# First rows of the relation table made in the front stage, and pair members of the table's sort copied to PSUM

## The chip, the cores and the metric

The kernel runs on one core of a Trainium2 chip. The metric is device time in microseconds (us), taken over several executions; lower is better. Five engines matter: TensorE (PE, with its weight loads PEld), VectorE (DVE), ScalarE (ACT), GpSimd (POOL) and SyncE (SP). SP and POOL issue the DMAs.

## The reference

Four residual blocks are applied in turn to node features x of 6,250 nodes by 256. The part that this change touches is the first block, a sum over 200,000 edges of relation-specific products:

```
# x: (6250, 256); src, dst, edge_type: (200000,); weight: (8, 256, 256)
x1  = layernorm(x)
hx  = einsum('ni,rio->rno', x1, weight)          # one product per node and relation
msg = hx[edge_type, src]
agg = segment_sum(msg, dst, 6250)
x   = x + agg * sqrt(0.5) + h_bias + (x1 @ loop_weight) * sqrt(0.5)
# second block: graph attention over 131,072 other edges (edge_index) picks
# 2 of 4 experts per node; it needs those edges ordered by their destination
# third block: gather and sum of a sparsified table over the same 200,000 edges
# fourth block: attention over 64 slice tokens
```

`dst` comes sorted and lies denser at low node numbers. The second block's edges come unsorted, so the kernel sorts them.

## The kernel before

The program is a chain of stages, each a block of five instruction streams, one for each engine. A stage ends with a barrier of all engines, so the last engine to finish sets its end. Within a stream the order is fixed by the code; engines meet through semaphores only. Nodes are handled in NW = 49 windows of P = 128 rows. Two stages matter here.

**front** loads x in 7 runs of 7 windows, normalises it in place in `b.x` (6 windows of each run on ACT, line 268, and one on POOL, line 253), writes the normalised rows to DRAM (`rows1`, SP line 224) and loads the three matrices of weights (lines 219 and 220). DVE meanwhile turns the lists of edges into tables: it takes the lowest and highest destination of each group (lines 301 to 331), TensorE spreads these over all partitions (lines 275 and 277), and DVE derives slots and masks from them (lines 336 to 375). When a run of rows has been written, POOL clears it in `b.x` (line 258), because `b.x` later serves as accumulator. The first DIRECT = 2 windows of run 0 are left for the next stage.

**relation_table** has three jobs that run beside each other.

- The table. For each window TensorE transposes the rows (`turn`, line 740), ACT copies them to `r_xt` (790), TensorE multiplies them by the 8 relation matrices in OUTS = 4 chunks of 128x512 (`multiply`, 747), ACT evacuates each chunk into `r_stage` (798), and SP stores the window, 1 MB, into `table1` (545). The rows come back from DRAM by `bring`, but for the first two windows, which are read from `b.x`. There are 3 PSUM banks for the products.
- Early edges. For the first edges (528 tiles of 128 edges less SKIP = 128, so 400 tiles), POOL gathers 128 rows for each tile with an indirect DMA into a ring of 8 (568). A 128x128 one-hot matrix is made by DVE for even tiles (702) and by ACT for odd ones (806, 809). TensorE multiplies the two into `r_sums` (758), and after each group of 4 tiles DVE adds the sums into `b.x` and `b.counted` (`add`, 695 and 697).
- The sort of the second block's 131,072 edges, a bitonic network over `r_keys`, two SBUF tensors of 128x1024 float32 used in turn. A stage compares the lower and the upper member of each pair. `mixed_stage` (422, 423) has four instructions of 128x256, `rising_stage` (433, 434) two of 128x512; both read both members from SBUF. There are 45 mixed and 108 rising stages. Fourteen times the keys are transposed by TensorE into the PSUM tensors `r_flipped` (`flip`, 766), and DVE brings them back (655, 676).

What sets the order: TensorE goes through the 196 chunks (49 windows by 4), and after each chunk takes about two gather tiles (`tiles_at`). DVE loops over the 400 tiles and does one step of the sort at tile `step_at(n)`, every 9/5 tiles, from tile 9 on; three steps after each request for a flip hold no work while it is made. ACT goes with the chunks: copy, evacuate, one-hot for tiles 7 ahead.

Names: `Chain` counts instructions of DVE in a semaphore, and `settled` waits for all of them. `b.written[j]` is raised when run j of the rows is in DRAM, `b.weighted` when the weights are in SBUF.

## Time and profile before

| what | value |
|---|---|
| median of 3 runs | 4322.95 us (4322.5 to 4335.69) |
| the profiled execution | 4332.92 us |
| its span, first to last instruction | 4331.0 us |
| TensorE busy over the span | 3673.5 us (85%) |
| POOL busy over the span | 2853.3 us (66%) |
| VectorE busy over the span | 2720.7 us (63%) |
| front: last clearing by POOL ends | 56.7 us after the start |
| relation_table: first product of TensorE | 59.9 us |
| next stage: first instruction of POOL | 643.5 us |

The profile page gives for each group of instructions the time busy, the mean of one, and the idle time just before them with what ended it. "DMA r_ring" as releaser means that TensorE stood until gathered rows had arrived. On POOL an indirect DMA counts as busy while the engine makes its descriptors; "issue" behind it is time in which it waited for nothing that the profile shows. Start times are from the start of the span. Neighbouring matmuls overlap in the records, so a period is best taken from start to start.

### The profile page before, as it was taken

What the parts mean: (1) busy time and instruction counts of PE and PEld (TensorE: products, weight loads), DVE (VectorE), ACT (ScalarE), POOL (GpSimd) and SP (SyncE); (2) the same over time, 40 slices, a digit from 0 to 9 for tenths busy, and PEclk for the clock granted to TensorE, in tenths of its full rate; (3) what the DMA queues carried; (4) which work ended last, traced back from release to release, by engine and by line L of the source; (5) the groups of instructions that cost most, each with busy time, mean ns of one, the idle gap of its engine ahead of it and who ended that gap; (6) DMA issues with size and microseconds to landing.
All of it is one profiled execution on the core that took longest, in us unless ns stands there. A gap on an engine that the chain in (4) does not pass through costs nothing. (4 is left out here: it accounts for less than half of the span.)

```text
span 4331.0 us, 73886 instructions
## 1 busy us (share of the span) xinstructions
PE 3673.5 (85%) x19739; PEld 2738.8 (63%) x19739; DVE 2720.7 (63%) x9585; ACT 1662.1 (38%) x3894; POOL 2853.3 (66%) x2874
## 2 busy tenths in 40 slices
PE   3999987777788878887699999978769999996988
PEld 2555554454455556646588888866358888884657
DVE  8766657666544443345555455557978888886862
ACT  3444444433233333323344444436523333333320
POOL 6877777777777777772677777742667777672230
PEclk9999997878799999965899999989879999997998
DMA  7555564333444443531433333336379999993001
GB/s 260 173 202 194 201 201 118 110 111 112 118 130 131 132 123 105 164 105 35 97 67 68 68 69 68 68 106 206 121 291 384 373 375 385 365 383 88 1 1 60
DMA packets 361677, 689.27 MB, mean 159 GB/s; under 512 B 70002, under 2 KB 188160, under 8 KB 354909
## 3 DMA queue, kind: packets, MB, share of 16 engines
q0 software_dynamic: 133184, 338.60, 26.0%
q1 hardware_dynamic: 228095, 345.94, 23.4%
q8 instruction: 179, 2.93, 0.3%
q14 instruction: 219, 1.79, 0.1%
HBM read 571.95 MB, written 112.35 MB: 158 GB/s over the span
## 5 line engine op out<-in xcount | busy, mean ns | idle before, releaser
L1102 POOL DMA_INDIRECT e_ring<-table,erow x1040 | 1007.0, 968 | 317.1 <-issue 177.5
L1553 PE MATMUL e_sums<-e_ring,e_onehot 128*128 128x257 f32 x2080 | 782.4, 480 | 290.1 <-DMA e_ring<-table,erow 252.1
L2652 POOL DMA_INDIRECT t_source<-source_rows,t_index x632 | 605.2, 958 | 207.2 <-issue 156.1
L1553 PEld LDWEIGHTS e_sums<-e_ring,e_onehot 128*128 128x128 f32 x2080 | 367.3, 219 | 527.3 <-issue 311.4
L1665 POOL DMA_INDIRECT e_ring<-table,esrc x544 | 535.6, 985 | 207.4 <-issue 134.8
L568 POOL DMA_INDIRECT r_ring<-rows,esrc x400 | 454.3, 1136 | 123.1 <-issue 85.0
L1068 ACT ACTIVATE k_sign<-ramp,low 128x128 bf16<-128x128 f32 x1024 | 361.5, 395 | 443.4 <-PE e_sums L1507 425.2
L1750 PE MATMUL e_total<-e_loads,e_times 128*128 128x256 f32 x3072 | 501.9, 299 | 17.2 <-DMA e_loads<-table 11.9
L1750 PEld LDWEIGHTS e_total<-e_loads,e_times 128*128 128x128 f32 x3072 | 408.7, 190 | 68.1 <-issue 35.6
L1648 ACT ACTIVATE e_times<-e_tally 128x320 fp32r<-128x320 f32 (+4 forms) x640 | 260.0, 427 | 483.1 <-PE e_tally L1734 479.2
L2836 PE MATMUL t_raw<-big,t_w 128*128 128x256 f32 x1600 | 374.8, 388 | 19.3 <-ACT t_hidden L2671 18.7
L1337 DVE SCALAR_TENSOR_TENSOR big<-e_sums,within,big 128x257 f32 x130 | 63.0, 485 | 494.1 <-PE e_sums L1553 492.4
L747 PE MATMUL r_product<-weights,r_xt 128*128 128x512 f32 x784 | 372.5, 598 | 0.0
L2847 PE MATMUL t_out<-t_w,t_hidden 128*128 128x256 f32 x1600 | 368.1, 383 | 0.0
L1692 DVE TENSOR_SCALAR e_place<-e_rampw,ddst 128x128 bf16<-128x128 f16 (+4 forms) x1024 | 340.1, 334 | 0.0
L2836 PEld LDWEIGHTS t_raw<-big,t_w 128*128 128x128 f32 x1600 | 299.5, 192 | 64.2 <-ACT t_hidden L2671 25.7
L1690 DVE TENSOR_SCALAR e_row<-e_rampr,dsrc 128x128 bf16<-128x128 bf16 x1024 | 270.4, 266 | 97.4 <-PE e_tally L1734 86.5
L2847 PEld LDWEIGHTS t_out<-t_w,t_hidden 128*128 128x128 f32 x1600 | 297.6, 190 | 37.3
L1411 DVE TENSOR_SCALAR e_onehot<-ramp,edst 128x128 f32<-128x128 f32 x1040 | 252.1, 299 | 17.7 <-DVE d_keys L1124 0.5
L1734 PE MATMUL e_tally<-e_place,e_row 128*128 128x128 bf16 (+4 forms) x1280 | 259.7, 300 | 0.0
L758 PE MATMUL r_sums<-r_ring,r_onehot 128*128 128x257 f32 x800 | 217.0, 387 | 33.2 <-DMA r_ring<-rows,esrc 32.0
L758 PEld LDWEIGHTS r_sums<-r_ring,r_onehot 128*128 128x128 f32 x800 | 149.7, 192 | 150.7 <-issue 119.9
(564 smaller groups left out, 6467.0 us busy)
## 6 DMA issues: line engine op xcount, KB each, us to landing
e_loads<-table SPq DMA_DIRECT2D x512, 256.0 KB
table<-r_stage SPq DMA_DIRECT2D x49, 1024.0 KB
outputs<-first_outputs SPq DMA_DIRECT2D x49, 512.0 KB, 6.5
first_outputs<-t_stage SPq DMA_DIRECT2D x96, 256.0 KB
t_near<-near_rows SPq DMA_DIRECT2D x79, 256.0 KB
e_ring<-table,erow POOLq DMA_INDIRECT x1040, 2.8
table<-n_split SPq DMA_DIRECT2D x49, 256.0 KB
t_source<-source_rows,t_index POOLq DMA_INDIRECT x632
```

The lines of the kernel that those rows point to most:

```text
L568: eng.indirect_dma_start(ring[:, t % RING, 0:D], None, m["rows1"], bass.IndirectOffsetOnAxis(ap=b.esrc[:, SKIP + t:SKIP + t + 1], axis=0)) ...
L747: mm = eng.matmul(product[n % BANKS][:, :], xt[w % 2][:, k, :], b.weights[:, k, 2 * c:2 * c + 2, :].rearrange("p r o -> p (r o)"), start=( ...
L758: eng.matmul(sums[g % 2][:, 0:ACCW], onehot[t % RING][:, :], ring[:, t % RING, :], start=(t % EGROUP == 0), stop=(t % EGROUP == EGROUP - 1 ...
L1068: eng.activation(sign[t % SIGNS][:, :], b.ramp[:, 0:P], ACT.Sign, bias=b.low[:, t:t + 1], scale=1.0).then_inc(signed, 1)
L1102: eng.indirect_dma_start(ring[:, t % RING, 0:D], None, table, bass.IndirectOffsetOnAxis(ap=b.erow[:, EARLY + t:EARLY + t + 1], axis=0)).th ...
L1553: eng.matmul(sums[g % SUMS][:, 0:ACCW], onehot[t % ONEHOTS][:, :], ring[:, t % RING, :], start=(t % GROUP == 0), stop=(t % GROUP == GROUP ...
L1665: eng.indirect_dma_start(ring[:, t % RING, :, :].rearrange("p n d -> p (n d)").bitcast(F32), None, halves, bass.IndirectOffsetOnAxis(ap=b. ...
L1692: eng.tensor_scalar(place[(2 * g + two) % MARKS][:, 0:wide(g) * P], rampw[:, 0:wide(g) * P], b.ddst[:, column(tile):column(tile) + 1], Non ...
L1750: mm = eng.matmul(part(n, q), times[g % TIMES][:, q * P:(q + 1) * P], loads[:, g % AHEAD, half, :], start=False, stop=False, skip_group_ch ...
L2652: eng.indirect_dma_start(source[s][:, q, :], None, a.source_rows, bass.IndirectOffsetOnAxis(ap=index[s][:, q:q + 1], axis=0)).then_inc(gat ...
L2836: mm = eng.matmul(raw[g][:, j % 2, :], w1[:, e, k, j * P:(j + 1) * P], b.xt[:, k, bass.ds(w * P, PAIR)], start=(k == 0), stop=(k == KH - 1))
L2847: mm = eng.matmul(out[s][:, q, :], hidden[s][:, j, q * P:(q + 1) * P], w2[:, e, j, :], start=(j == 0), stop=(j == NB - 1))
```

## The change

**In front.** The two windows that are still in `b.x` are multiplied there. TensorE transposes both windows once ACT has normalised them, ACT copies them out of PSUM into `c_xt` after the first window of run 1, and TensorE makes 8 chunks of 128x512 into 5 PSUM banks: chunk 0 ahead of the two matmuls that spread the lists, chunks 1 to 7 behind them. ACT evacuates the chunks behind its last normalisation, into `stage` buffers that both stages now share. SP loads the first three windows' rows of the next stage once run 0 has been written, waits for four evacuations, stores window 0, waits for four more and stores window 1. POOL clears all of run 0, after the transposes. Some lists of the front are worked on in place (`einside` and `inside` over `erows` and `rows`, `slot` over `etype`, five small ones inside `esrc`), with a wait for all of DVE's previous instructions where an input is overwritten.

**In relation_table.** MADE = 47 windows are left, so 188 chunks; the 400 tiles are spread over these. The first evacuations wait for front's stores. The two windows cleared by DVE (line 713) fall away.

**In the sort.** Before each of the 153 stages ACT copies the upper members of all pairs, 128x512, from `r_keys` into the PSUM tensor `r_flipped0` (`halve`), and DVE compares the lower members in SBUF with that copy. The copy waits until DVE has finished the step before; DVE waits for the copy. `halve` stands in ACT's stream AHEAD = 2 tiles ahead of the tile at which DVE does the step before, behind the evacuation and the one-hot of that chunk.

```diff
+MADE = NW - DIRECT
+HELD = 3
+OUTS = RELS * D // BANK
...
+    BANKS = 5
+    CHUNKS = OUTS * DIRECT
...
+        xt = sb("c_xt", [P, DIRECT, KH, P])
...
-        einside = sb("c_einside", [EROWS, 2, EGROUP * P])
+        einside = erows.bitcast(F32)
...
+        product = [ctx.enter_context(nc.psum_tensor(f"c_product{n}", [P, BANK], F32)) for n in range(BANKS)]
...
+            eng.wait_ge(b.written[0], 16)
+            for i in range(HELD):
+                eng.dma_start(b.xw[i][:, :], m["rows1"][(DIRECT + i) * P:(DIRECT + i + 1) * P, :]).then_inc(b.brought[i], 16)
+            for w in range(DIRECT):
+                eng.wait_ge(evacuated, OUTS * (w + 1))
+                eng.dma_start(m["table1"][w * P:(w + 1) * P, :], b.stage[w][:, :]).then_inc(b.stored[w], 16)
...
-                low = DIRECT if j == 0 else RUN * j
-                eng.memset(b.x[:, low:RUN * (j + 1), :], 0.0).then_inc(emptied, 1)
+                if j == 0:
+                    eng.wait_ge(transposed, 1)
+                eng.memset(b.x[:, RUN * j:RUN * (j + 1), :], 0.0).then_inc(emptied, 1)
...
+                if w == RUN:
+                    eng.wait_ge(transposed, 1)
+                    eng.activation(xt[:, :, :, :].rearrange("p w k n -> p (w k n)"),
+                                   turned[:, :, :, :].rearrange("p w k n -> p (w k n)"), ACT.Copy).then_inc(copied, 1)
+            for n in range(CHUNKS):
+                w, c = divmod(n, OUTS)
+                eng.wait_ge(multiplied, n + 1)
+                eng.activation(b.stage[w][:, c * BANK:(c + 1) * BANK], product[n % BANKS][:, :], ACT.Copy).then_inc(evacuated, 1)
...
+            def multiply(n):
+                w, c = divmod(n, OUTS)
+                wait_if(eng, evacuated, n - BANKS + 1)
+                for k in range(KH):
+                    mm = eng.matmul(product[n % BANKS][:, :], xt[:, w, k, :],
+                                    b.weights[:, k, 2 * c:2 * c + 2, :].rearrange("p r o -> p (r o)"),
+                                    start=(k == 0), stop=(k == KH - 1))
+                mm.then_inc(multiplied, 1)
+
             eng.wait_ge(filled, FILLED)
+            eng.wait_ge(normed[0], DIRECT)
+            for w in range(DIRECT):
+                for k in range(KH):
+                    mm = eng.transpose(turned[:, w, k, :], b.x[:, w, k * P:(k + 1) * P], b.ident[:, :])
+            mm.then_inc(transposed, 1)
+            eng.wait_ge(copied, 1)
+            eng.wait_ge(b.weighted, 16 * (KH + 1))
+            multiply(0)
             eng.wait_ge(ranged, RANGED)
             eng.matmul(eacross[:, :, :, :].rearrange("p q c r -> p (q c r)"), b.ones[0:EROWS, :],
                        elaid[:, :, :, :].rearrange("r q c e -> r (q c e)"), start=True, stop=True).then_inc(spread, 1)
             eng.matmul(across[:, :, :, :].rearrange("p q c r -> p (q c r)"), b.ones[0:GROWS, :],
                        laid[:, :, :, :].rearrange("r q c e -> r (q c e)"), start=True, stop=True).then_inc(spread, 1)
+            for n in range(1, CHUNKS):
+                multiply(n)
...
             v.did(eng.tensor_reduce(elowest[:, :], erows[:, :, :], AX_X, ALU.min))
+            v.settled()
             v.did(eng.scalar_tensor_tensor(einside[:, :, :], erows[:, :, :], float(N), erows[:, :, :], ALU.is_lt, ALU.mult))
...
+    def halved(self):
+        self.stages += 1
+        self.v.eng.wait_ge(self.copied, self.stages)
...
+def mixed_stage(eng, keys, order, half, k, j):
 
     v = order.v
     cut = lambda t: t[:, :].rearrange("p (a u b o c) -> p a u b o c", u=2, b=1 << (k - 1 - j), o=2, c=1 << j)
     source, target = cut(keys[order.at]), cut(keys[1 - order.at])
+    above = half[:, :].rearrange("p (a u b c) -> p a u b c", u=2, b=1 << (k - 1 - j), c=1 << j)
+    order.halved()
     v.settled()
     for u in range(2):
-        first, second = source[:, :, u, :, 0, :], source[:, :, u, :, 1, :]
+        first, second = source[:, :, u, :, 0, :], above[:, :, u, :, :]
         v.did(eng.tensor_tensor(target[:, :, u, :, u, :], first, second, ALU.min))
         v.did(eng.tensor_tensor(target[:, :, u, :, 1 - u, :], first, second, ALU.max))
     order.turn()
...
+def rising_stage(eng, keys, order, half, reach):
 
     v = order.v
     cut = lambda t: t[:, :].rearrange("p (a o c) -> p a o c", o=2, c=reach)
     source, target = cut(keys[order.at]), cut(keys[1 - order.at])
+    above = half[:, :].rearrange("p (a c) -> p a c", c=reach)
+    order.halved()
     v.settled()
-    v.did(eng.tensor_tensor(target[:, :, 0, :], source[:, :, 0, :], source[:, :, 1, :], ALU.min))
-    v.did(eng.tensor_tensor(target[:, :, 1, :], source[:, :, 0, :], source[:, :, 1, :], ALU.max))
+    v.did(eng.tensor_tensor(target[:, :, 0, :], source[:, :, 0, :], above, ALU.min))
+    v.did(eng.tensor_tensor(target[:, :, 1, :], source[:, :, 0, :], above, ALU.max))
     order.turn()
...
+    AHEAD = 2
+    halves_at = {}
+    for stage_of in table_stages():
+        halves_at.setdefault(max(0, step_at(stage_of[0] - 1) - AHEAD), []).append(stage_of)
+    sorted_to = {}
...
+                eng.wait_ge(transposed, w - HELD + 1)
+                eng.dma_start(xw[w % HELD][:, :], rows[DIRECT + w]).then_inc(brought[w % HELD], 16)
...
-            for w in range(DIRECT, DIRECT + HELD):
-                eng.dma_start(xw[w % HELD][:, :], rows[w]).then_inc(brought[w % HELD], 16)
             eng.dma_start(m["scr_edst"], b.edst[:, :]).then_inc(kept, 16)
-            for w in range(NW):
+            for w in range(MADE):
                 eng.wait_ge(evacuated, (w + 1) * OUTS)
-                eng.dma_start(table[w], stage[w % 2][:, :]).then_inc(stored[w % 2], 16)
-                if DIRECT + HELD <= w + HELD < NW:
+                eng.dma_start(table[DIRECT + w], stage[w % 2][:, :]).then_inc(stored[w % 2], 16)
+                if w + HELD < MADE:
...
+            half = flipped[0]
...
-            eng.wait_ge(transposed, DIRECT)
-            eng.memset(b.x[:, 0:DIRECT, :], 0.0).then_inc(zeroed, 1)
...
-                    wait_if(eng, stored[w % 2], 16 * (w // 2))
+                    eng.wait_ge(stored[w % 2], 16 * (w // 2 + 1))
...
+            def halve(step, at, reach):
+                eng.wait_ge(sorting, sorted_to[step - 1])
+                eng.activation(flipped[0][:, :].rearrange("p (a c) -> p a c", c=reach),
+                               keys[at][:, :].rearrange("p (a o c) -> p a o c", o=2, c=reach)[:, :, 1, :],
+                               ACT.Copy).then_inc(halved, 1)
...
                     for t in tiles_at(step_of(w, c), RING - 1):
                         if t % 2 == 1:
                             match(t)
+                    for t in tiles_at(step_of(w, c), 0):
+                        for stage_of in halves_at.get(t, ()):
+                            halve(*stage_of)
+            for t in range(TILES - TAIL, TILES):
+                for stage_of in halves_at.get(t, ()):
+                    halve(*stage_of)
```

TensorE from its first instruction on. Before, front holds the two matmuls that spread the lists, and relation_table opens with the transposes of the windows in `features` (that is `b.x`):

```order
L275 MATMUL c_eacross<-c_elaid,ones 128x264
L277 MATMUL c_across<-c_laid,ones 128x392
L117 UNCONDITIONAL_BRANCH
L730 UNCONDITIONAL_BRANCH
L740 MATMUL r_turned<-ident,features 128x128 x4
L747 MATMUL r_product<-weights,r_xt 128x512 x2
```

The changed kernel's TensorE from its first instruction on:

```order
L310 MATMUL c_turned<-ident,features 128x128 x4
L301 MATMUL c_product<-weights,c_xt 128x512 x2
L316 MATMUL c_eacross<-c_elaid,ones 128x264
L318 MATMUL c_across<-c_laid,ones 128x392
L301 MATMUL c_product<-weights,c_xt 128x512 x14
L120 UNCONDITIONAL_BRANCH
L820 UNCONDITIONAL_BRANCH
L826 MATMUL r_turned<-ident,rows_in 128x128 x4
L833 MATMUL r_product<-weights,r_xt 128x512 x2
```

Four transposes and one chunk now stand ahead of the matmuls that spread the lists, and seven chunks behind them.

ACT in relation_table while the sort runs. Before (evacuation, then the two instructions of a one-hot):

```order
L798 ACTIVATE r_stage<-r_product 128x512
L806 ACTIVATE r_away<-ramp,edst 128x128
L809 ACTIVATE r_onehot<-r_away,ones 128x128
L798 ACTIVATE r_stage<-r_product 128x512
L806 ACTIVATE r_away<-ramp,edst 128x128
L809 ACTIVATE r_onehot<-r_away,ones 128x128
```

The changed kernel's ACT at the same kind of place:

```order
L899 ACTIVATE r_flipped<-r_keys 128x512
L883 ACTIVATE stage<-r_product 128x512
L891 ACTIVATE r_away<-ramp,edst 128x128
L894 ACTIVATE r_onehot<-r_away,ones 128x128
L899 ACTIVATE r_flipped<-r_keys 128x512
L883 ACTIVATE stage<-r_product 128x512
```

One copy of pair members has come in behind nearly every evacuation and one-hot.

DVE between two additions of sums, early in the sort. Before:

```order
L702 TENSOR_SCALAR r_onehot<-ramp,edst 128x128
L422 TENSOR_TENSOR r_keys<-r_keys 128x128x2
L423 TENSOR_TENSOR r_keys<-r_keys 128x128x2
L422 TENSOR_TENSOR r_keys<-r_keys 128x128x2
L423 TENSOR_TENSOR r_keys<-r_keys 128x128x2
L702 TENSOR_SCALAR r_onehot<-ramp,edst 128x128
```

The changed kernel's DVE there:

```order
L794 TENSOR_SCALAR r_onehot<-ramp,edst 128x128
L475 TENSOR_TENSOR r_keys<-r_keys,r_flipped 128x128x2
L476 TENSOR_TENSOR r_keys<-r_keys,r_flipped 128x128x2
L475 TENSOR_TENSOR r_keys<-r_keys,r_flipped 128x128x2
L476 TENSOR_TENSOR r_keys<-r_keys,r_flipped 128x128x2
L794 TENSOR_SCALAR r_onehot<-ramp,edst 128x128
```

The order is the same; the second operand now comes from `r_flipped`.

## Rows read from the trace of the kernel before

**Rows 1.** The page's costliest groups: busy, mean ns, idle before and releaser.

```profile
L568 POOL DMA_INDIRECT r_ring<-rows,esrc x400 | 454.3, 1136 | 123.1 <-issue 85.0
```

**Rows 2.** Waits in 57 to 644 us: us in total, times, longest.

```profile
PE r_sums L758 <- DMA r_ring<-rows,esrc: 32.0, 32, 2.3
...
POOL r_ring L568 <- PE r_sums L758: 37.1, 120, 0.6
```

**Rows 3.** Timeline of TensorE with a flip and a turn: start, length, then the instruction.

```profile
486.56 1.04 PE L766 MATMUL r_flipped<-ident,r_keys 128*128 128x128 f32 x8
487.43 0.60 PE L758 MATMUL r_sums<-r_ring,r_onehot 128*128 128x257 f32 x2
487.86 1.88 PE L747 MATMUL r_product<-weights,r_xt 128*128 128x512 f32 x4
489.58 1.03 PE L758 MATMUL r_sums<-r_ring,r_onehot 128*128 128x257 f32 x4
490.45 0.38 PE L740 MATMUL r_turned<-ident,r_xw 128*128 128x128 f32 x2
490.67 1.88 PE L747 MATMUL r_product<-weights,r_xt 128*128 128x512 f32 x4
```

**Rows 4.** Timeline of POOL: one gather beside line 655, one beside a stage.

```profile
288.39 0.94 POOL L568 DMA_INDIRECT r_ring<-rows,esrc  x1 [0.30 <-issue]
...
294.56 2.13 POOL L568 DMA_INDIRECT r_ring<-rows,esrc  x1 [0.30 <-issue]
```

**Rows 5.** Timeline of DVE over the same time.

```profile
287.83 1.29 DVE L655 TENSOR_TENSOR r_keys<-r_flipped,r_change 128x512 f32<-128x512 f32 x2 [6.34 <-PE r_flipped L766]
...
293.34 0.48 DVE L695 SCALAR_TENSOR_TENSOR features<-r_sums,ewithin,features 128x256 f32 x1
...
294.57 0.69 DVE L433 TENSOR_TENSOR r_keys<-r_keys 128x512 f32<-128x512 f32 x1
295.18 0.69 DVE L434 TENSOR_TENSOR r_keys<-r_keys 128x512 f32<-128x512 f32 x1
```

**Rows 6.** POOL's groups by line, 611 to 643 us and 660 to 800 us.

```profile
L568 POOL DMA_INDIRECT r_ring<-rows,esrc x20 | 19.0, 950 | 6.1 <-issue 4.3 <-PE r_sums L758 1.8
...
L1102 POOL DMA_INDIRECT e_ring<-table,erow x111 | 106.7, 962 | 33.8 <-issue 18.3 <-PE e_sums L1553 15.5
```

**Rows 7.** Timeline at the start of relation_table: TensorE's products and DVE.

```profile
59.93 3.04 PE L747 MATMUL r_product<-weights,r_xt 128*128 128x512 f32 x4
...
63.30 0.69 DVE L583 TENSOR_SCALAR r_keys<-r_ends 128x1024 int32<-128x1024 int32 x1 [2.20 <-DMA r_ends<-in_gdst_cols]
...
68.41 3.62 PE L747 MATMUL r_product<-weights,r_xt 128*128 128x512 f32 x4
...
73.03 1.88 PE L747 MATMUL r_product<-weights,r_xt 128*128 128x512 f32 x4
```

**Rows 8.** Timeline at the end of relation_table.

```profile
631.72 3.49 PE L758 MATMUL r_sums<-r_ring,r_onehot 128*128 128x257 f32 x14
...
643.51 0.13 POOL L1094 MEMSET e_ring<- 128x17 f32 x1 [7.86 <-POOLq L120]
```

**Rows 9.** Timeline of front on TensorE, DVE and POOL.

```profile
40.24 1.22 PE L275 MATMUL c_eacross<-c_elaid,ones 66*128 66x264 f32 x2 [40.24 <-DVE c_elaid L331]
...
42.98 1.17 POOL L258 MEMSET features<- 128x1280 f32 x1 [1.41 <-DMA rows<-features]
...
45.38 0.29 DVE L351 CAST c_ebasis<-c_eacross 128x132 int32<-128x132 f32 x1
...
54.85 1.88 POOL L258 MEMSET features<- 128x1792 f32 x1 [0.78 <-DMA rows<-features]
```

**Rows 10.** Timeline of the next stage's sort, in which ACT already copies pair members.

```profile
711.54 0.42 DVE L1118 TENSOR_TENSOR d_keys<-d_keys,d_half 128x256 f32<-128x256 f32 x1
712.05 0.60 ACT L1019 ACTIVATE d_half<-d_keys 128x512 f32<-128x512 f32 x1 [3.16 <-DVEq L1160]
...
712.79 0.42 DVE L1117 TENSOR_TENSOR d_keys<-d_keys,d_half 128x256 f32<-128x256 f32 x1
```

More of the change, by code:

```diff
@@ L460, in table_asked, with table_stages @@
     return asked
+def table_stages():
+    stages, step, at = [], 3, 0
+    for k in range(1, LOGF):
+        for j in range(k - 1, -1, -1):
+            stages.append((step, at, 1 << j))
+            step, at = step + 1, 1 - at
+    step, at = step + 1, 1 - at
+    for j in range(LOGF - 1, -1, -1):
+        stages.append((step, at, 1 << j))
+        step, at = step + (j > 0), 1 - at
+    for k in range(LOGF + 1, LOGE + 1):
+        for reaches in ([1 << (j - LOGF) if j >= LOGF else P << (j - 7) for j in range(k - 1, 6, -1)],
+                        [1 << j for j in range(6, -1, -1)]):
+            step, at = step + 3, 1 - at
+            for reach in reaches:
+                step += 1
+                stages.append((step, at, reach))
+                at = 1 - at
+    return stages
 def relation_table(nc, b, m):
-    OUTS = RELS * D // BANK
     BANKS = 3
@@ L488, in relation_table @@
         pb = lambda name: ctx.enter_context(nc.psum_tensor(name, [P, BANK], F32))
[L489 removed]
+        xw, stage, brought, stored = b.xw, b.stage, b.brought, b.stored
         xt = [sb(f"r_xt{s}", [P, KH, P]) for s in range(2)]
[L491 removed]
         keys = [sb(f"r_keys{s}", [P, FLAT]) for s in range(2)]
@@ L507, in relation_table @@
         numbered = sem("r_numbered")
-        brought = [sem(f"r_brought{s}") for s in range(HELD)]
         transposed = sem("r_transposed")
@@ L512, in relation_table @@
         evacuated = sem("r_evacuated")
-        stored = [sem(f"r_stored{s}") for s in range(2)]
         zeroed = sem("r_zeroed")
@@ L607, in sort @@
                 v.settled()
+                sorted_to[step] = v.n
                 step += 1
@@ L626, in sort @@
                     for j in range(k - 1, -1, -1):
-                        mixed_stage(eng, keys, order, k, j)
+                        mixed_stage(eng, keys, order, half, k, j)
+                        sorted_to[step] = v.n
                         step += 1
@@ L632, in sort @@
                 order.turn()
+                sorted_to[step] = v.n
                 step += 1
@@ L635, in sort @@
                 for j in range(LOGF - 1, 0, -1):
-                    rising_stage(eng, keys, order, 1 << j)
+                    rising_stage(eng, keys, order, half, 1 << j)
+                    sorted_to[step] = v.n
                     step += 1
                     yield
-                rising_stage(eng, keys, order, 1)
+                rising_stage(eng, keys, order, half, 1)
                 for k in range(LOGF + 1, LOGE + 1):
@@ L678, in sort @@
                     for j in range(6, -1, -1):
+                        sorted_to[step] = v.n
                         step += 1
                         yield
-                        rising_stage(eng, keys, order, 1 << j)
+                        rising_stage(eng, keys, order, half, 1 << j)
                 v.settled()
@@ L770, in _ @@
             turn(0)
-            eng.wait_ge(b.weighted, 16 * (KH + 1))
-            for w in range(NW):
+            for w in range(MADE):
                 eng.wait_ge(copied, w + 1)
-                if w + 1 < NW:
+                if w + 1 < MADE:
                     turn(w + 1)
@@ L814, in _ @@
                 match(t)
-            for w in range(NW):
-                if w + 1 < NW:
+            for w in range(MADE):
+                if w + 1 < MADE:
                     copy(w + 1)
@@ L3869, in build @@
                 b.spans = fb("spans", [P, DLOWS], I32)
-                front(nc, b, m)
                 b.low = fb("low", [P, GT])
                 b.high = fb("high", [P, GT], BF16)
-                relation_table(nc, b, m)
+                b.brought = [first.semaphore(f"brought{s}") for s in range(HELD)]
+                b.stored = [first.semaphore(f"stored{s}") for s in range(2)]
+                with ExitStack() as made:
+                    mb = lambda name, shape: made.enter_context(nc.sbuf_tensor(name, shape, F32))
+                    b.xw = [mb(f"rows_in{s}", [P, D]) for s in range(HELD)]
+                    b.stage = [mb(f"stage{s}", [P, RELS * D]) for s in range(2)]
+                    front(nc, b, m)
+                    relation_table(nc, b, m)
                 relation_rows = table1.rearrange("n (r d) -> (n r) d", d=D)
```

64 lines of the change are left out of this document (34 added, 30 removed).

## The prediction

> **What bounds the kernel now.** I read the waits of relation_table first, because the change is worth something only where it shortens what ends last there. TensorE waits for one thing alone, gathered rows: 32.0 us in 32 waits [rows 2]. POOL, which makes those gathers, is never kept waiting: its longest wait for TensorE is 0.6 us, which is hardly more than the gap of 0.3 us that stands between any two gathers [rows 2, 4]. Its 400 gathers are 454.3 us busy with 123.1 us of such gaps, 577 us together or 1.44 us a tile [rows 1]. That is the whole length of the stage: from TensorE's first product at 59.93 to the next stage at 643.51 are 583.6 us [rows 7, 8].
>
> TensorE is nearly as full. From start to start a chunk takes 1.72 us (487.86 to 489.58), two gather tiles 0.87, a turn of a window 0.22, a flip 0.87 (486.56 to 487.43) [rows 3]. So its work is 196 x 1.72 = 337.1, 400 x 0.435 = 174.0, 14 x 0.87 = 12.2, 47 x 0.22 = 10.3: together 533.6 us. Of 583.6 us it loses 50.0. At the start, 59.93 to 73.03, it does two chunks and four tiles, 5.2 us of 13.1, and loses 7.9 [rows 7]. At the end, 631.72 to 643.51, it does eight tiles, 3.5 us of 11.8, and loses 8.3 [rows 8]. The middle loses 33.8, mostly the waits for gathers. So two engines share the bound: TensorE by its work, and POOL by holding it up.
>
> **Why POOL is slow here.** A gather takes 0.95 us when DVE sorts nothing (20 gathers late in the stage, mean 950 ns [rows 6]). In the stage as a whole the mean is 1136 ns [rows 1]. The single rows show when: the gather at 294.56 takes 2.13 us, and it runs beside a rising stage at 294.57, both of whose inputs are in SBUF [rows 4, 5]. The gather at 288.39 takes 0.94 us beside line 655, which has the same shape and also writes SBUF, but reads one input from PSUM [rows 4, 5]. That is the form that all 153 stages are to have. The next stage of the kernel sorts with one operand in PSUM throughout, and its gathers have a mean of 962 ns [rows 6, 10].
>
> The Trainium skill speaks on both sides here. Its page "SBUF — State Buffer", section "Who interferes with whom", says that a tensor_tensor with both inputs in SBUF contends with GpSimd's reads, but infers that descriptor generation is not stalled by it, since that needs the write side of the shared ports. By the second sentence the copies would bring nothing. The two gathers just compared do not agree with it, so I weigh it as a rival and no more.
>
> **Part 1, two windows fewer in relation_table.** 8 chunks x 1.72 and two turns x 0.22 (47 down to 45 once the first two are left at the head) leave TensorE 14.2 us: 519.4 in place of 533.6. Alone this would bring nearly nothing, because POOL's 577 us stay.
>
> **Part 2, pair members in PSUM.** POOL at 0.96 + 0.31 = 1.27 us a tile needs 508 us for 400 gathers. TensorE now needs 519.4 / 400 = 1.30 us a tile. POOL falls behind it by a small margin and TensorE becomes the only bound. The middle loss of 33.8 us goes, but for two things. DVE's own integer work on the keys at the start still has two SBUF inputs, some 4 us on about four gathers, which the ring of eight mostly hides: I count 1 us. The other is the chain below.
>
> **Part 3, the price of the copies.** ACT gets 153 copies of 128x512, for which no row before has the direction from SBUF to PSUM; the nearest, PSUM to SBUF of the same size, is 0.60 us [rows 10]. Together 92 us on an engine that mostly waits for TensorE's chunks, so their sum costs nothing. What can cost is the new ring of waits: DVE stage, ACT copy, DVE stage. In the next stage, from the start of the last compare (711.54) to the first of the following stage (712.79) are 1.25 us where 0.33 would do, so a copy opens a hole of 0.92 us [rows 10]. DVE fills it with a one-hot or an addition if one is due. An addition with its one-hot takes 1.23 us (293.34 to 294.57) [rows 5], with the second one-hot (I take 0.2 us, half of what one instruction of 128x256 takes) 1.43 in every 4 tiles. A mixed stage is 4 x 0.33 = 1.32, a rising one 2 x 0.61 = 1.22 (294.57 to 295.18 is 0.61) [rows 5]. A step comes every 1.8 tiles, which TensorE passes in 2.34 us. A step without an addition takes 1.32 + 0.92 = 2.24; one with an addition (45%) 1.32 + 1.43 = 2.75; the mean is 2.47 for mixed and 2.37 for rising stages. Over 45 mixed stages this is 6 us too much, over the ten rising ones that follow nothing to speak of, and later groups have empty steps to recover in. So 6 us; the bounds are 0, if the slack of two tiles takes it up, and the fully serial case of the first rival. DVE's wait for the copy holds its one-hots and additions behind it, on which TensorE's gather tiles wait; ACT's wait for DVE holds the next evacuation and copy behind it. Both have about two tiles in hand.
>
> **Part 4, the front.** TensorE is idle in it until 40.24 us [rows 9], so the chunks lie beside other work unless they end last. The weights are ahead of the rows on the same queue, and the first run of rows has been written by 42.98 [rows 9]: I take them as there at about 40.5. Chunk 0 costs 3.0 to 3.6 us there, as the first ones after an idle stretch do [rows 7], the two spreading matmuls then end at about 46.5, where DVE needs them at 45.38 [rows 9]: DVE is at most 1.2 us later, and has that in hand against POOL. Seven chunks behind: 7 x 1.72 = 12.0 if TensorE is at full rate, to 58.5, and if the first still goes at the slow rate 60.2. Evacuating the last adds 0.7. POOL, which ends the front now, is done at 56.73 (54.85 + 1.88) [rows 9]. So the front ends 2.5 to 4.2 us later: I take 3. If all seven go at the slow rate, 7 x 3.6, it ends 15 later. The transposes and their copy hold ACT's normalising up by 0.6 us, which the queue of writes hides. SP's loads of three windows only move from one stage to the other; the two stores, 2 MB, are new just there, and the key lists of the sort (DVE waits for them until 63.30 [rows 7]) and the first gathers come in behind them: 2 us more lost at the start. The in-place lists and their waits cost tenths on DVE, hidden by POOL.
>
> **The sum.** relation_table after: 519.4 work, 7.9 + 2.0 at the start, 7.0 in the middle, 6.0 at the end (gathers are ahead now, so the last eight tiles don't wait for them, but the last store of 1 MB still has to land): 542.3 us against 583.6, so 41.3 less. With the front's 3 more the gain is 38 us. All other stages are the same. The profiled execution of 4332.92 goes to 4295; that one lies 10 us above the median, so I forecast 4322.95 - 38 = 4285 for the median, with 4274 (nothing lost in the chain, a little less at both ends) to 4297 (the front wholly at the slow rate).
>
> **Rivals.** *The chain of copies sets the pace* (slower side). If DVE reaches each stage before its copy has begun and never fills the hole, a step is the plain sum: 0.64 (1.43 x 1.8 / 4) for the other work, so 1.32 + 0.92 + 0.64 = 2.88 mixed and 2.78 rising, against 2.34. 45 x 0.54 + 108 x 0.44 = 72 us in place of 7, and the time would be 4285 + 65 = 4350. It is slower than before from 0.29 us lost per stage on. For it speaks that ACT's stream holds the copy behind an evacuation that waits for TensorE. Against it, the next stage fills the hole with one-hots, and the copy stands two tiles ahead: 7%. *Half of that*, copies late in every other step: some 36 us in place of 7, 4314: 15%, with 4298 to 4325 as its range.
>
> *The gathers stay slow*, because something other than the operand's place lengthens them (the page's rule above would do that). POOL's 577 us stay, the stage only moves with the front: 4322.95 + 3 = 4326. Against it stand the paired rows: 7%. *More gain*, if TensorE's loss at both ends shrinks as well: below 4274, 6%. The forecast keeps 65%.
>
> **How the numbers follow.** A measurement of this kernel can tell about 0.3%, 13 us, from no change. Faster than 4310: the forecast, the larger gain and nearly two thirds of the half-late case, 0.65 + 0.06 + 0.10 = 0.81. Within 0.3%: the rest of that case and the slow gathers, 0.13 with a little of the first rival's lower end. Slower: 0.06. The range 4270 to 4316 takes in the forecast's own, nearly all of the larger gain and the likelier half of the half-late case, 8 in 10.
>
> **What the changed profile should show.** The gathers of relation_table at a mean of 0.96 to 1.0 us, none of 2 us beside a stage, and POOL with real waits for TensorE. TensorE's waits for gathers under 8 us. First product of the stage near 63 us, next stage near 605. DVE with waits for the copy into `r_flipped` that are long (over 1 us) in few places; if their sum in the first 100 tiles passes 30 us and TensorE waits for DVE's one-hots or additions, the chain is the bound and the prediction is wrong. If the gathers stay at 1.1 us, it is wrong at its root. In the front, the last evacuation should end near 59.5 us.

## The result and the profile after

The changed kernel takes 4293.28 us (median of 4 executions, 4290.7 to 4296.03) against 4323.89 for the kernel before on the same chip (4 executions, 4322.5 to 4335.69): ratio 0.9924, 95% interval 0.9909 to 0.9939, that is 26 to 39 us faster. A second comparison gave 0.9921 (0.9907 to 0.9934). The forecast was 4285, with a range of 4270 to 4316.

| | before | after |
|---|---|---|
| profiled execution | 4332.92 us | 4293.01 us |
| span | 4331.0 us | 4291.2 us |
| relation_table: first product | 59.93 | 62.12 |
| next stage: first instruction of POOL | 643.51 | 604.52 |
| length between the two | 583.6 us | 542.4 us |
| gathers of that stage, busy in sum | 454.3 us | 381.9 us |

The page's group of the gathers, which answers to [rows 1] (busy, mean ns, idle before, releaser):

```profile
L645 POOL DMA_INDIRECT r_ring<-rows,esrc x400 | 381.9, 955 | 153.5 <-issue 79.0
```

A gather takes 955 ns in the mean where it took 1136. From 80 us to the end of the stage no gather took more than 1.22 us; in the kernel before 46 took over 1.5 us and one 4.31.

The traces also show what a long gather waits for. All 46 in the kernel before end 0.82 us (within 0.02) after the last compare of some stage of the sort, where of its 239 gathers of at most 1.0 us 2 do. The second gather of [rows 4], beside the compares of [rows 5], is one of them: the last compare ends at 295.87 (295.18 + 0.69) and the gather at 296.69 (294.56 + 2.13). So a gather that meets a stage can stand until its last compare is over. In the kernel before the 193 gathers that meet a compare in their first 0.94 us took 1.32 us in the mean and the 192 others 0.95; in the changed kernel the 266 that meet one took 0.95, like the others. One stage early in the sort of the changed kernel, with a gather beside it:

```profile
85.84 0.94 POOL L645 DMA_INDIRECT r_ring<-rows,esrc  x1 [0.30 <-PE r_sums L844]
```

```profile
85.54 0.62 DVE L475 TENSOR_TENSOR r_keys<-r_keys,r_flipped 128x256 f32<-128x256 f32 x1
86.07 0.63 DVE L476 TENSOR_TENSOR r_keys<-r_keys,r_flipped 128x256 f32<-128x256 f32 x1
```

The waits of relation_table, 60 to 600 us, which answer to [rows 2]:

```profile
PE r_sums L844 <- DMA r_ring<-rows,esrc: 9.6, 3, 6.0
PE r_sums L844 <- DVE counted L789: 3.8, 4, 1.9
...
POOL r_ring L645 <- PE r_sums L844: 73.4, 143, 2.9
...
DVE r_keys L488 <- ACT r_flipped L899: 71.5, 68, 4.0
...
DVE r_keys L475 <- ACT r_flipped L899: 14.2, 25, 1.2
```

TensorE's waits for gathered rows went from 32.0 to 9.6 us, and of those 9.3 are one wait at the start and one in the last tiles. POOL now has a wait of up to 2.9 us, where none was over 0.6: TensorE is the only bound. The 86 us for which DVE waits for copies (71.5 + 14.2) are new. They lie in time that DVE spent before in waiting for TensorE, for sums and flips: 199 us in the kernel before, 58 in the changed one.

Busy time by stretch, columns in the order PE, PEld, DVE, ACT, POOL, granted clock, share of DMA, GB/s. The changed kernel:

```profile
75.00:217.00 142.00, 140.24 (x451) 81.98 (x450) 120.73 (x375) 100.67 (x229) 102.99 (x108) 1.00 0.62 207
217.00:580.00 363.00, 359.85 (x1235) 217.36 (x1234) 245.53 (x636) 230.88 (x532) 256.27 (x271) 1.00 0.61 203
```

The kernel before, in the same stretches:

```profile
75.00:217.00 142.00, 126.31 (x390) 70.40 (x389) 104.64 (x339) 62.79 (x150) 115.17 (x89) 0.99 0.51 172
217.00:580.00 363.00, 352.33 (x1198) 209.77 (x1196) 235.36 (x610) 173.09 (x414) 284.39 (x258) 1.00 0.59 198
```

POOL put out 108 gathers in the first stretch where it had put out 89, in less busy time. TensorE was 89% busy there and is now 99%.

The front on TensorE, with the first instructions of relation_table, which answers to [rows 7] and [rows 9]:

```profile
40.84 3.75 PE L301 MATMUL c_product<-weights,c_xt 128*128 128x512 f32 x4 [8.24 <-DMA loopw<-in_loop_weight]
44.39 1.09 PE L316 MATMUL c_eacross<-c_elaid,ones 66*128 66x264 f32 x2
45.27 1.19 PE L318 MATMUL c_across<-c_laid,ones 98*128 98x392 f32 x2
46.29 12.18 PE L301 MATMUL c_product<-weights,c_xt 128*128 128x512 f32 x28
...
62.12 1.88 PE L833 MATMUL r_product<-weights,r_xt 128*128 128x512 f32 x4
70.03 2.05 PE L844 MATMUL r_sums<-r_ring,r_onehot 128*128 128x257 f32 x4 [6.03 <-DMA r_ring<-rows,esrc]
```

The weights arrive at 40.8, chunk 0 goes slowly, chunks 1 to 7 take 12.18 us, and the first gather tile waits until 70.03.

### The profile page after: what moved, and what is told of

It is laid out like the page before. It is cut to its first block and busy times, and to the rows that moved or that the text cites. A ratio compares the mean times of both kernels' runs of the same rounds, so it can differ in the third digit from the quotient of the medians.

```text
span 4291.2 us, 74189 instructions
## 1 busy us (share of the span) xinstructions
PE 3660.0 (85%) x19739; PEld 2737.3 (64%) x19739; DVE 2721.9 (63%) x9584; ACT 1740.4 (41%) x4046; POOL 2773.2 (65%) x2874
## 5 line engine op out<-in xcount | busy, mean ns | idle before, releaser
L1650 PE MATMUL e_sums<-e_ring,e_onehot 128*128 128x257 f32 x2080 | 767.1, 472 | 300.1 <-DMA e_ring<-table,erow 247.2
L2749 POOL DMA_INDIRECT t_source<-source_rows,t_index x632 | 604.5, 957 | 208.4 <-issue 157.8
L645 POOL DMA_INDIRECT r_ring<-rows,esrc x400 | 381.9, 955 | 153.5 <-issue 79.0
L833 PE MATMUL r_product<-weights,r_xt 128*128 128x512 f32 x752 | 354.1, 593 | 0.0
L1859 PE MATMUL e_sums<-e_ring,e_onehot 128*128 128x256 f32 x1088 | 202.4, 284 | 45.0 <-DMA e_ring<-table,esrc 44.9
```

The source lines that it names most:

```text
L645: eng.indirect_dma_start(ring[:, t % RING, 0:D], None, m["rows1"], bass.IndirectOffsetOnAxis(ap=b.esrc[:, SKIP + t:SKIP + t + 1], axis=0)) ...
L833: mm = eng.matmul(product[n % BANKS][:, :], xt[w % 2][:, k, :], b.weights[:, k, 2 * c:2 * c + 2, :].rearrange("p r o -> p (r o)"), start=( ...
L1650: eng.matmul(sums[g % SUMS][:, 0:ACCW], onehot[t % ONEHOTS][:, :], ring[:, t % RING, :], start=(t % GROUP == 0), stop=(t % GROUP == GROUP ...
L2749: eng.indirect_dma_start(source[s][:, q, :], None, a.source_rows, bass.IndirectOffsetOnAxis(ap=index[s][:, q:q + 1], axis=0)).then_inc(gat ...
```

## The experiments

All times are medians; ratios are to the kernel before on the same chip. "Stage" is the length from TensorE's first product in relation_table to the end, and "end" is the first instruction of the next stage in the trace, 643.5 before and 604.5 in the changed kernel. It is a sharper measure than the whole time, of which the kernel before alone had executions from 4320.01 to 4340.69 (23 of them, median 4329.48).

### The kernel before once more

No edit.

> The kernel before, unchanged, profiled once more. The first profiled execution of it took 4332.9 us where three of its four other executions took 4322.5 to 4324.8, and its relation_table stage ran from TensorE's first product at 59.9 to the next stage at 643.5, 583.6 us. Theory (the table stage is held by POOL's gathers, whose length depends on how they fall beside DVE's compares, so it is this stage that varies from run to run): if this execution is near 4323, the stage is shorter by most of the 10 us, near 574, and the gathers' sum near 445 us in place of 454. Rival (the 10 us lie in another stage): the stage again takes 583 us in a run of 4323.

Measured: the profiled execution took 4325.55 us, and its stage ran from 59.95 to 645.4, 585.4 us, with 454.1 us of gathers. The execution was 7 us shorter than the first profiled one and its stage 2 us longer. The theory fell: most of what varies from run to run lies outside this stage. The time after this stage was 3687.5 us in the first execution (4331.0 - 643.5), 3677.6 in this one, and 3686.7 in the changed kernel's.

### The front alone

```diff
-    order.halved()
...
-        first, second = source[:, :, u, :, 0, :], above[:, :, u, :, :]
+        first, second = source[:, :, u, :, 0, :], source[:, :, u, :, 1, :]
...
-                            halve(*stage_of)
```

(Likewise in `rising_stage`.)

> The changed kernel's front and 47 windows, but the compares read both members from SBUF again and no copies are made. Theory (POOL's gathers beside compares with two SBUF inputs are the bound): gathers stay at about 1.13 us mean, POOL shows no real waits, TensorE's waits for gathers grow from 32 to over 40 us, and the whole is worth 0 to 3 us: 4321 to 4326. Rival (TensorE's work is the bound and the 14 us taken from it come through): 4310 or less.

Measured: 4325.4 us (ratio 0.9988, interval 0.9978 to 0.9997), end 639.8, gathers 1120 ns, TensorE's waits for gathers 34.4 us. The theory holds for the time and the gathers: 14 us of TensorE's work are gone from the stage and about 4 to 6 come out at its end. The waits that were to grow past 40 us did not: 34.4 is what the kernel before had in its second profile (34.9).

### The copies alone

The kernel before with `halve`, `halved`, `table_stages` and the compares of the changed kernel; front and 49 windows as before.

> The kernel before with the copies of pair members to PSUM alone; front and 49 windows as before. Theory: gathers at 0.95 us, TensorE is the only bound with 533.6 us of work, so the stage takes about 533.6 + 8 at the start + 8 at the end + 5 = 555 us in place of 574 to 584; time 4323 minus 16 to 20 = 4303 to 4307 (the front ends 2.5 us earlier than in the changed kernel, and lacks its 14 us saved). Rival (the two parts only work together, or the copies give all): 4293 or 4318 and over.

Measured: 4297.79 us (ratio 0.9919, interval 0.9904 to 0.9934), stage 549.3 us, end 609.15. The stage is 6 us shorter than the 555 us expected, and the gain of 32 us on the whole is more than the 16 to 20 expected, in part because I had set the kernel before at 4323 us. The page's group of the gathers:

```profile
L605 POOL DMA_INDIRECT r_ring<-rows,esrc x400 | 381.4, 954 | 160.3 <-PE r_sums L810 86.2
```

From 75 to 580 us TensorE is busy for all of the 505 us; the middle, for which I had set 5 us, loses nothing. The copies give 34 of the trace's 39 us (643.5 to 609.15), the front the last 4.6.

### All copies and waits, but the operand in SBUF

```diff
-        first, second = source[:, :, u, :, 0, :], above[:, :, u, :, :]
+        first, second = source[:, :, u, :, 0, :], source[:, :, u, :, 1, :]
...
-    v.did(eng.tensor_tensor(target[:, :, 0, :], source[:, :, 0, :], above, ALU.min))
+    v.did(eng.tensor_tensor(target[:, :, 0, :], source[:, :, 0, :], source[:, :, 1, :], ALU.min))
...
```

(Likewise the instruction with `ALU.max`.)

> The changed kernel with all its copies and waits, but the compares read the upper member from SBUF as before, not the copy in PSUM. Theory (only the place of the second operand matters): gathers are slow again, 1.1 us mean or more with single ones of 2 us; TensorE waits for gathers some 40 us; 4321 to 4330, the copies and their waits adding 0 to 5 us to the front-only kernel. Rival (the spacing that the copies put between compares is what lets the gathers through): gathers at 0.95 to 1.0 us and 4293 to 4300.

Measured: 4309.98 us (ratio 0.9947, interval 0.9934 to 0.9961), end 625.2, between the two expectations. The group of the gathers:

```profile
L645 POOL DMA_INDIRECT r_ring<-rows,esrc x400 | 428.9, 1072 | 127.1 <-issue 89.9
```

Its timeline early in the sort, POOL and then DVE:

```profile
86.45 0.95 POOL L645 DMA_INDIRECT r_ring<-rows,esrc  x1 [0.30 <-PE r_sums L844]
87.70 2.24 POOL L645 DMA_INDIRECT r_ring<-rows,esrc  x1 [0.30 <-issue]
90.25 0.96 POOL L645 DMA_INDIRECT r_ring<-rows,esrc  x1 [0.30 <-issue]
```

```profile
86.70 0.64 DVE L475 TENSOR_TENSOR r_keys<-r_keys 128x256 f32<-128x256 f32 x1
87.23 0.63 DVE L476 TENSOR_TENSOR r_keys<-r_keys 128x256 f32<-128x256 f32 x1
87.77 0.63 DVE L475 TENSOR_TENSOR r_keys<-r_keys 128x256 f32<-128x256 f32 x1
88.31 0.62 DVE L476 TENSOR_TENSOR r_keys<-r_keys 128x256 f32<-128x256 f32 x1
88.84 0.29 DVE L794 TENSOR_SCALAR r_onehot<-ramp,edst 128x128 f32<-128x128 f32 x1
89.63 0.43 DVE L475 TENSOR_TENSOR r_keys<-r_keys 128x256 f32<-128x256 f32 x1 [0.51 <-ACT r_flipped L899]
```

The gather at 87.70 ends at 89.94, a microsecond after the last of the four compares (88.31 + 0.62) and 0.81 us after the one-hot behind them (88.84 + 0.29). Of the 23 gathers over 1.5 us in this kernel the other 22 end 0.82 us after the last compare of a stage, as those of the kernel before do. The compares are not held up in turn. That the four shown take 0.62 to 0.64 us, where later ones take 0.42, belongs to this first stage of the sort: the same four take 0.62 to 0.64 in the changed kernel, as its rows above show for two. Over all stages the first compare of a rising stage takes 692 ns in the mean here and 686 in the changed kernel.

The only difference to the changed kernel is where one operand lies, and with it in PSUM no gather beside the sort exceeds 1.22 us. That the operand's place matters is shown; it is worth 20.7 us at the end (625.2 to 604.5) and 13 to 17 us in the timed runs (4309.98 against 4297.32 and 4293.28). The other 14.6 us between the front alone (639.8) and this kernel come with the copies even though nobody reads them: they put holes between the stages of DVE. Gathers over 1.5 us after 80 us number 41 with the front alone and 23 here. That the holes are what lets the gathers through fits both traces, since a gather goes on when a stage is over, but it was not tried by itself.

### The changed kernel once more

No edit.

> The changed kernel, unchanged, beside the kernel before on one chip with more executions. Theory (the trace's 39 us, of which the copies alone gave 34 and the front 5): ratio 0.990 to 0.992, about 5 us below the kernel with the copies alone (4298). Rival (the front's part is lost again elsewhere): the same time as the copies alone.

Measured: 4297.32 us (4289.68 to 4300.93), ratio 0.9921 (0.9907 to 0.9934), end 605.4. The whole times of this kernel and of the one with the copies alone cannot be told apart (ratios 0.9924 and 0.9921 against 0.9919); only the ends in the traces can, 604.5 and 605.4 against 609.15. That the front's 5 us reach the whole time is not shown by the timed runs.

### Where the copy stands in ACT's stream

```diff
-    AHEAD = 2
+    AHEAD = 4
```

and, in two further kernels, 0 and 6.

> AHEAD 4 in place of 2: each copy of pair members stands two tiles earlier in ScalarE's stream. In the changed kernel TensorE loses 3.8 us in four waits for VectorE's additions and about 3 us in small ones, which the kernel with the copies alone does not have, and VectorE waits 86 us for copies. Theory (copies come late for VectorE because they stand too late): VectorE's waits for copies fall under 50 us, TensorE's losses to additions go, 3 to 5 us faster. Rival (the copy waits for VectorE's step before, not for its turn): ScalarE stands longer at the copy, its evacuations come later, same time or up to 5 us slower.

> AHEAD 0 in place of 2: each copy stands two tiles later in ScalarE's stream, at the tile at which VectorE does the step before. AHEAD 4 ended the stage 5 us earlier than AHEAD 2 and halved VectorE's waits for copies in rising stages from 71 to 35 us. Theory (where the copy stands sets how late VectorE is, and TensorE pays once the slack of two tiles is gone; the slower rival of the prediction): VectorE's waits for copies over 130 us, TensorE's waits for additions and one-hots over 30 us, 20 to 60 us slower than the changed kernel, so 4315 to 4355, with gathers still at 0.95 us. Rival (a chain of waits is bounded by its own length, wherever the copy stands): within 5 us of 4297.

> AHEAD 6. Theory: VectorE can only be four to seven tiles ahead of TensorE, so ScalarE now comes to the copy before VectorE has done the step before and stands there; its evacuations and one-hots come late. TensorE's losses grow again, to 5 to 30 us more than with AHEAD 4: next stage at 605 or later. Rival (three banks and eight one-hots in hand cover it): 598 to 600 as with AHEAD 4.

| AHEAD | median, ratio (interval) | stage, end | DVE's waits for copies (rising, mixed) | TensorE's waits for DVE |
|---|---|---|---|---|
| 0 | 4378.06, 1.011 (1.0095 to 1.0126) | 624.5, 686.7 | 138.5, 37.2 | 68.0 |
| 2 | 4297.32, 0.9921 (0.9907 to 0.9934) | 542.7, 605.4 | 71.3, 14.2 | 3.7 |
| 4 | 4290.99, 0.9906 (0.9893 to 0.992) | 537.6, 599.4 | 35.1, 13.0 | 0.8 |
| 6 | 4292.06, 0.9917 (0.9903 to 0.9931) | 537.8, 600.0 | 29.4, 12.7 | none |

AHEAD 4 did as expected in the trace: DVE's waits for copies in sum fell under 50 us, and the end came 5 to 6 us earlier. The timed runs don't separate 2, 4 and 6, whose intervals overlap. AHEAD 0 took 81 us more than AHEAD 2, where 20 to 60 were expected, and is 49 us slower than the kernel before on its chip (4328.98): the slower rival of the prediction is real, and begins within two tiles of where the change stands. TensorE's waits in that kernel:

```profile
PE r_sums L844 <- DVE counted L789: 57.1, 38, 2.7
PE r_sums L844 <- DVE r_onehot L794: 10.9, 11, 3.5
PE r_sums L844 <- DMA r_ring<-rows,esrc: 9.6, 2, 6.0
```

and its gathers, as fast as ever, so that what it loses does not come from them:

```profile
L645 POOL DMA_INDIRECT r_ring<-rows,esrc x400 | 381.4, 953 | 236.1 <-PE r_sums L844 157.3
```

The mechanism can be seen in the changed kernel itself, at the longest of its few such waits. ACT, then DVE, then TensorE:

```profile
430.61 0.60 ACT L883 ACTIVATE stage<-r_product 128x512 f32<-128x512 f32 x1 [2.08 <-PE r_product L833]
431.10 0.39 ACT L891 ACTIVATE r_away<-ramp,edst 128x128 f32<-128x128 f32 x1
431.59 0.40 ACT L894 ACTIVATE r_onehot<-r_away,ones 128x128 f32<-128x128 f32 x1
431.89 0.39 ACT L891 ACTIVATE r_away<-ramp,edst 128x128 f32<-128x128 f32 x1
432.37 0.40 ACT L894 ACTIVATE r_onehot<-r_away,ones 128x128 f32<-128x128 f32 x1
432.68 0.58 ACT L899 ACTIVATE r_flipped<-r_keys 128x512 f32<-128x512 f32 x1
```

```profile
428.02 1.29 DVE L767 COPY r_keys<-r_flipped 128x512 f32<-128x512 f32 x2 [3.13 <-PE r_flipped L852]
433.29 0.69 DVE L488 TENSOR_TENSOR r_keys<-r_keys,r_flipped 128x512 f32<-128x512 f32 x1 [3.98 <-ACT r_flipped L899]
```

```profile
433.43 0.60 PE L844 MATMUL r_sums<-r_ring,r_onehot 128*128 128x257 f32 x2
435.93 0.46 PE L844 MATMUL r_sums<-r_ring,r_onehot 128*128 128x257 f32 x1 [1.90 <-DVE counted L789]
```

DVE's keys are ready at 429.3. ACT waits 2.08 us for a chunk, evacuates it and makes two one-hots before it copies at 432.68. DVE stands 3.98 us, the addition behind the stage is late, and TensorE waits 1.90 us for it. With AHEAD 4 or 6 the copy stands before that evacuation. My theory for AHEAD 6 fell: ACT does stand longer at the copies (128 us in place of 78 with AHEAD 4), but it had waited for products anyway (37 us are left of 84), and TensorE waits for evacuations only 1.3 us in all.

### A slower pace of the sort

```diff
-    step_at = lambda n: RING + 1 + (n - TABLE_FIRST) * STEPPED // 5
+    step_at = lambda n: RING + 1 + (n - TABLE_FIRST) * 19 // 10
```

> One step of the sort every 19/10 tiles in place of 9/5; all else as in the changed kernel. The last step moves from tile 363 to about 383 of 400. Theory (a step with its copy takes VectorE about as long as TensorE's 1.8 tiles, so additions come late now and then): with 5% more time a step the waits of TensorE for additions (3.8 us and some small ones) vanish, 3 to 6 us faster. Rival (those losses come from somewhere else than the pace of the sort): same time.

Measured: 4297.19 us (ratio 0.9922), end 606.25, DVE's waits for copies 77.5 + 16.7, TensorE's waits for DVE 5.0. The theory fell: more time for a step does not help. With the table above this says that a copy is late through its place in ACT's stream and not because DVE has too much to do.

### The front's stores later

```diff
-            for w in range(DIRECT):
-                eng.wait_ge(evacuated, OUTS * (w + 1))
-                eng.dma_start(m["table1"][w * P:(w + 1) * P, :], b.stage[w][:, :]).then_inc(b.stored[w], 16)
+            eng.wait_ge(evacuated, OUTS * DIRECT)
...
             eng.dma_start(ends[:, 1, :], m["gdst_cols"]).then_inc(keyed, 16)
+            for w in range(DIRECT):
+                eng.dma_start(table[w], stage[w][:, :]).then_inc(stored[w], 16)
```

> The stores of the two windows made in front (2 MB) are issued at the head of relation_table, behind the loads of the sort's key lists, not in front. In the changed kernel the first gathered rows reach TensorE at 70.0, 8 us after the gather was begun at 61.9 (6 us after 59.2 in the kernel before), and VectorE has the key lists at 67.7 (63.3 before). Theory (both wait behind the two stores): key lists at about 65, first gathered rows at 67 to 70, 1 to 3 us faster. Rival (the gathers wait behind any 2 MB, now the same bytes later): key lists earlier, gathers the same, no change in time.

Measured: 4290.84 us (ratio 0.9907, interval 0.9892 to 0.9923), end 606.4. The key lists come at 65.5 in place of 67.7, the first gathered rows at 68.5 in place of 70.0, and the stage still ends no earlier. Its third chunk starts at 75.6, 75.2 in the changed kernel: the rows came earlier, but the second chunk took 3.62 us in place of 2.60, at a granted clock of 0.64 between 72 and 76 us in place of 0.84. The lower time of the timed runs is not borne out by the trace, and its interval overlaps that of the changed kernel (0.9907 to 0.9934).

> AHEAD 4 and the two stores of front issued behind the key lists' loads together. Theory (the two don't touch each other; the late stores end front 1 us earlier and gave nothing behind it): next stage at 599 to 600, ratio to before 0.989 to 0.991, as with AHEAD 4 alone. Rival (the timed runs of the late stores, 6 us lower than the changed kernel's, were no chance): 4286 or less.

Both edits together: 4290.46 us (ratio 0.9917, interval 0.9903 to 0.993), end 598.1. As AHEAD 4 alone within what can be measured.

### The copies alone with AHEAD 4

> The kernel with the copies alone, front as before and 49 windows, with AHEAD 4. With AHEAD 2 it left TensorE no middle loss. Theory (its 14 us more of work cover the late copies): same as with AHEAD 2, next stage at 608 to 610, about 4298, so that with AHEAD 4 the front's part is worth 8 to 10 us in place of 5. Rival (AHEAD 4 takes something of its own from TensorE's stream): 603 to 605.

Measured: 4301.17 us (ratio 0.9936, interval 0.9922 to 0.995), end 609.55. As expected: without the front's part the earlier copies bring nothing, since TensorE had no loss to give back. With AHEAD 4 in both kernels the front's part is worth 10.2 us at the end (609.55 to 599.4); with AHEAD 2 it was worth 4.6. The timed runs point the same way (4301.17 against 4292.06 and 4290.46 for the two kernels with the front's part on the same chip), but the intervals just overlap.

## Why the prediction was right, and where it was off

**What bounds, and why POOL was slow.** Right, and now shown by the runs: gathers at 955 ns (0.96 was set), and TensorE as the only bound. The front alone brought little, as Part 1 said. Compares with both inputs in SBUF do lengthen a gather: 1072 ns in the mean with the operand put back, 955 without. Two signs of the changed profile came out otherwise: TensorE's waits for gathers were to be under 8 us and were 9.6, because of the last tiles, and DVE's waits for copies over 1 us were to be few and were 33 of 93. The section "Who interferes with whom" of the page "SBUF — State Buffer" of the Trainium skill, which infers that they don't stall the making of descriptors, is not borne out by these runs. What it says of instructions of GpSimd that read SBUF would fit, if such a gather counts as one; no run shows what the gather reads there.

**The stage.** The sum was 542.3 us, measured 542.4. That is closer than its terms deserve, and luck: three terms were off by -2.0, -1.5 and +3.6 us, and the errors cancel.

| term | predicted | measured |
|---|---|---|
| work of TensorE | 519.4 | 519.4 by the same rates |
| lost at the start, to the third chunk | 9.9 | 7.9 (62.12 to 75.18, less 5.2) |
| lost in the middle | 7.0 | 5.5 (the rest: 542.4 less the other three) |
| lost at the end, from the last product | 6.0 | 9.6 (591.4 to 604.52, less 3.5) |

The end was mis-sized. I took the last gathers to be far ahead; but POOL, now held by TensorE, can issue the last one only 8 tiles ahead, at 595.32, and its rows came at 598.88, 3.3 us waited for, with the last stores of the table and of the sorted keys issued just before. At the start, the first gathered rows did come late behind the stores (70.0 in place of 65.2), but the next tiles then waited no more: the kernel before had a second wait of 1.5 us and two chunks of over 3 us there.

**The chain.** I put its cost of 6 us into the 45 mixed stages, by adding a fixed hole of 0.92 us to steps without an addition. The mixed stages cost about 1 us (TensorE's waits for DVE up to 200 us are 1.1), and most of the rest came singly in rising stages (three waits of 2.9 us in all, the longest 1.9), where the copy stood behind a late evacuation. The mechanism named in the first rival, a copy behind an evacuation that waits for TensorE, was the right one, while the mean over steps in Part 3 was not what sets the price. The 7% for that rival were fair for AHEAD 2, but I had no point from which it decides in terms of the code: it is between AHEAD 2 and 0.

**The front.** First product at 62.1, predicted near 63. Weights at 40.8 (40.5), chunk 0 3.75 (3.0 to 3.6), the other seven 12.18 (12.0), all at the full rate.

**The whole time.** The forecast was 4285 and the median is 4293.28, 8 us above it and well inside the range. 38 us of gain were predicted; the end of the stage moved by 39 to 40 us (643.5 and 645.4 to 604.5 and 605.4), and the timed runs gained 30.6 and 31.8. One step is off for certain: I took 10 us off the profiled execution because it lay 10 us above a median of three, and let the whole gain come off 4322.95. With 23 executions the median of the kernel before is 4329.48, so the profiled one was ordinary and that median of three 6.5 us low. 4293.28 lies 36 to 40 us under 4329.48 to 4332.92, but the repeat, 4297.32 against 4329.09 on one chip, gained only 31.8. "All other stages are the same" can't be checked to better than the spread there: the time after this stage was 3677.6 and 3687.5 us in the two profiled executions of the kernel before, 3686.7 and 3693.8 in those of the changed one. What it is that varies there stays open.

## What to carry to other kernels

Where POOL issues gathers beside VectorE, look at the length of single gathers, not at the share of POOL's busy time: a mean of 1.14 us made of many at 0.95 and some at 2 means that something holds them, and moving one operand of VectorE's two-input instructions to PSUM can free POOL even at the price of one more copy for each stage on an engine with time to spare. Such a copy needs its place in the copying engine's stream chosen by what stands before it: here two tiles later turned a gain of 0.8% into a loss of 1.1%, and two tiles earlier cost nothing. And when work is taken from the engine that bounds, check how far behind the next one is: the same 14 us were worth 4 to 6, 4.6 or 10.2 us depending on what else held TensorE.

## What the runs showed of the hardware

The hold-up goes one way. A gather beside compares with two SBUF inputs took up to 4.31 us in place of 0.95, and of the 110 over 1.5 us in the kernel before, the front alone and the kernel with the operand put back, 109 end 0.82 us after the last compare of a stage. The compares took the same in all of these: those of 128x512 have means of 686 to 692 ns with two SBUF inputs and 679 to 686 with one.

Two SBUF inputs are not the only form that can hold a gather. The changed kernel has one of 2.16 us beside integer instructions of DVE on 128x1024 that have one input, in SBUF; it ends 0.84 us after one of them:

```profile
77.98 2.16 POOL L645 DMA_INDIRECT r_ring<-rows,esrc  x1 [0.30 <-PE r_sums L844]
```

```profile
78.00 0.69 DVE L681 TENSOR_SCALAR r_ends<-low 128x1024 int32<-128x1024 int32 x1
78.61 0.69 DVE L682 TENSOR_SCALAR r_ends<-low 128x1024 int32<-128x1024 int32 x1
```

A copy by ACT of 128x512 float32 from SBUF to PSUM took 602 ns in the mean of 153, and one from PSUM to SBUF 592 in the mean of 188: the direction made no difference that matters here.
